# Fused rotation and DiT block on one core: the Exp table load moves by ten slots, V's zeroing moves to GpSimd, the gates' rows are spread by DMA

## The chip, the core and the metric

The kernel runs on one NeuronCore of a Trainium2 chip. The metric is device time in microseconds of one launch, taken several times; the median counts. A profiled execution of the same program is read beside it.

## What is computed

```python
# L0: x (2,1024,288), cond (2,288)
U, _ = qr(P)                                   # (288,64)
R = expm(skew(silu(cond) @ W.T + b))           # (2,64,64)
x = x + (z @ R - z) @ U.T                      # z = x @ U
# L1: a transformer block modulated by the same cond
ada = silu(cond) @ ada_w + ada_b               # (2, 6*288)
shift_msa, scale_msa, gate_msa, shift_mlp, scale_mlp, gate_mlp = split(ada, 6)
x = x + gate_msa * (attention(modulate(layernorm(x), shift_msa, scale_msa)) @ proj_w + proj_b)
x = x + gate_mlp * (gelu(modulate(layernorm(x), shift_mlp, scale_mlp) @ fc1_w + fc1_b) @ fc2_w + fc2_b)
```

In the attention each token is a set of 16 heads of 18 channels, and the softmax runs over the 16 heads of the same token (`nthd,ntkd->nthk`), so attention mixes heads within a token and no tokens with each other.

## The kernel before, in words

All five engines run lists written out by hand, tied by semaphores; each engine works its list strictly in order. The program has these stages.

- **Prologue (0 to about 107 us).** A loop of steps k builds the orthogonal basis pivot by pivot (VectorE's reciprocal, L1271, and two updates, L1273 and L1276; ScalarE's square root, L1037, and the scaled row, L1040), then the matrix exponential. Into the same steps "fillers" are laid: TensorE transposes of X, and the products `ada 0` and `ada 1` that give the modulation and the two gates; `fill_out` (L999) is ScalarE's copy of a filler's result out of PSUM, and counts `fill_done`. `ada 1` leaves the gates in `AD[:, 1, :]`: rows 0 and 1 the attention gate of the two batch rows, rows 32 and 33 the MLP gate. GpSimd splits the weights into f16 pairs meanwhile (L460 to L472) and then waits.
- **Rotation and first norms (107 to 120 us).** `delta` (L714) adds the rotation to X, VectorE takes mean and variance (L1319, L1321).
- **qkv (about 120 to 214 us).** NCH = 4 chunks of 512 tokens, NQ = 12 units each, so 48 units; a loop over slots `gu` runs on TensorE, ScalarE and VectorE, in the same order on each. In slot gu: `turn` pieces of the next chunk where TURN_AT says so (slots 5 to 7 for chunk 1, 14, 16, 18 for chunk 2, 26, 28, 30 for chunk 3): TensorE transposes (L739), ScalarE writes them twice (L1081, f32 and f16), VectorE subtracts (L1373, `split`). Then the unit itself: 7 matmuls (L815), ScalarE's copy `high` (L1098 or, for V, L1093), VectorE's remainder `low` (L1419). TensorE's unit gu waits for `low(gu-2)`. Then the slot's `job`s: 16 small matmuls (L799, L776) that turn the unit's heads, copied out by ScalarE (L1114, L1112); job i waits for the copy of job i-2. From slot 24 on, every third slot has a `maxima` (L763) with VectorE's reduction (L1378). Slots 31 to 34 and 37 to 40 have jobs; 35 has none and 36 has one short one (L769 on TensorE, L1105 on ScalarE). VectorE also makes `norm_var` (L1327), `norm_scales` (L1335 to L1343) and `source` (L1352, L1357: the normalised X) of the coming chunk: for chunk 1 in slots 0 to 3, and `turn(1)` in slot 5 waits for it.
- **The gates, before.** In slots 1 to 4 `gate` (L595) spreads one row of AD over 128 partitions by a matmul with a broadcast column of the identity, and `fill_out` copies and scales it (L1006): GATE0 (attention, two batch rows), then GATE (MLP). As soon as the two GATE0 copies are done, GpSimd folds the gate into proj's weights: WP, seven instructions for each batch row (L501 to L507), then GB2 (L513, L514). The projection (about 284 us) is the first reader of WP; GATE itself is first read by `result` (L1550) in the MLP.
- **The Exp table, before.** At `EXP_TABLE_AT` = 2 * NQ + 1 = 25 ScalarE applies Exp to one column (L1136) so that its table is loaded ahead of the softmax. It comes after the slot's jobs.
- **Attention (214 to 284 us).** Scores (L856), Exp (L1142), values (L893). V's groups lie in VG, the first 2048 columns of `scratch`, where the unused columns are zero and one column of each group is 1. VectorE zeroes it (L1450, L1452) after the last `low`; ScalarE's first copy into it (`v_out(0)`, L1151) waits for that. XN, the normalised X that `turn` reads, lay in the same place.
- **Projection, MLP (284 to 419 us).** L947, then L970 and L986, with TensorE busy nearly throughout.

SyncE issues all DMAs in one list: the loads, the 32 small copies that build the skew matrix, the broadcast of fc2's bias (L389, 144 KB from one DRAM row to 128 partitions, after a wait for `weights` 5), then the attention maxima and the outputs.

Of the kernel before, what the change touches and what calls it, by code (L numbers as in the profile page):

```python
# [6 lines left out]
F32 = mybir.dt.float32  # L7
# [5 lines left out]
B, T, D = 2, 1024, 288  # L13
R = 64
H, DH = 16, 18
MLP = 4 * D
P = 128
# [14 lines left out]
def build(nc, x, c, pmat, wskew, bskew, qkv_w, qkv_b, proj_w, proj_b, fc1_w, fc1_b, fc2_w, fc2_b, ada_w, ada_b, out):  # L32
    with ExitStack() as ctx:
# [131 lines left out]
        YT = big[:, 2 * (NF + 1) * CH:2 * (NF + 1) * CH + 6 * D].rearrange("p (a n) -> p a n", a=6)  # L165
        B2ALL = stage[:, NT * D:NT * D + D]
        GB2 = scratch[:, 8704:8704 + B * D].rearrange("p (b n) -> p b n", b=B)
        vd = nc.dram_tensor("skew_entries", [B, NSKEW], F32, kind="Internal").ap()


        in_p, in_c, in_w, in_br, in_ada, in_adab = (sem(n) for n in ("in_p", "in_c", "in_w", "in_br", "in_ada", "in_adab"))
        in_b2, x_bias = sem("in_b2"), sem("x_bias")
        in_wq, in_wp, in_w1, in_w2 = (sem(n) for n in ("in_wq", "in_wp", "in_w1", "in_w2"))
        in_x = [sem(f"in_x{i}") for i in range(NCH)]
        consts = sem("consts")
# [57 lines left out]
        ZT_AT = 34  # L233
        ADA_ROWS = ((0, 1, 3, 4), (2, 5))
        FG = len(work) - 1
        NFILL = FG + 5
        XDONE = [work.index((i + 2, 2)) + 1 for i in range(2)]
        pieces = []
        for n, w in enumerate(work):
# [72 lines left out]
        ROWS_LATER, ROWS_BANK = {4: 2, 8: 3}, {4: VB[0], 8: MXB[0]}  # L312
        PAIRED = 10
        DVE_AT = 17
        GATE_AT = 1
        EXP_TABLE_AT = 2 * NQ + 1
        NSLOT = 6 * 2 * NCH + 7 + 4
        assert max(slots) < NSLOT

# [27 lines left out]
        def _(sp):  # L347
# [39 lines left out]
            sp.wait_ge(weights, 5)  # L387
            src = bass.AP(tensor=fc2_b.tensor, offset=fc2_b.offset, ap=[[0, P], [1, D]])
            sp.dma_start(B2ALL, src).then_inc(in_b2, 16)  # L389

            def max_row(n):
                if n < 2:
# [18 lines left out]
        def _(pool):  # L411
# [83 lines left out]
                pool.memset(HT[96:P, a_, 4, :], FINE).then_inc(ht_ones, 1)  # L495
                pool.wait_ge(ht_ones, a_ + 1)
            pool.wait_ge(in_wp, 96)
            pool.wait_ge(fill_done, FG + 3)
            for b in range(B):
                r = slice(0, 98)  # L500
                chain(pool.tensor_tensor(WPG[:, 0:2, :], SWP[:, 0:2, :], GATE0[:, b, :].unsqueeze(1).broadcast_to([P, 2, D]), ALU.mult))  # L501
# [6 lines left out]
                pool.wait_ge(folded, 2 * b + 2)  # L508

            pool.wait_ge(in_b2, 16)  # L510
            pool.wait_ge(fill_done, NFILL)
            for b in range(B):
                chain(pool.tensor_scalar(GB2[:, b, :], GATE[:, b, :], FINE * FINE, None, ALU.mult))  # L513
                chain(pool.tensor_tensor(GB2[:, b, :], GB2[:, b, :], B2ALL, ALU.mult))  # L514
            for t in range(NT):
                pool.wait_ge(proj_mul, t + 1)
                pool.tensor_tensor(X[:, t, :], X[:, t, :], YT[:, t % 6, :], ALU.add).then_inc(x_mid, 1)  # L517
# [7 lines left out]
        def _(pe):  # L525
# [16 lines left out]
            def filler(n, p_):  # L542
# [42 lines left out]
                                       XT[0:k, b, c0:c0 + 2 * P], start=(b == 0), stop=(b == 2))  # L585
                if pieces[last_piece[n]] == (n, p_):
                    mm.then_inc(fill_ready, 1)

            def gate(n):

                f = MISC
                pe.wait_ge(fill_done, n)
                g, b = divmod(n - FG - 1, 2)
                row = 32 * g + b
                pe.matmul(f[:, 0:D], ident[0:R, row:row + 1].broadcast_to([R, P]), AD[0:R, 1, :], start=True, stop=True).then_inc(fill_ready, 1)  # L595

            def skew_matrix():

# [182 lines left out]
            def job(i):  # L781

                if i == 0:
                    pe.wait_ge(att_const, 1)
                    pe.wait_ge(fill_done, NFILL)
                if i >= 2:
                    pe.wait_ge(col_done, i - 1)
                out = CB[i % 2]
                if jobs[i][0] == "max":
                    max_turn(out, jobs[i][1]).then_inc(col_ready, 1)  # L790
                    return
                pr, w, q = jobs[i]
                pe.wait_ge(qk_low, 6 * pr + 3 + w + 1)
                if w == 2:
                    mm = v_columns(out, pr, q)
                else:
                    for hh in range(4):
                        for c_ in range(2):
                            mm = pe.matmul(out[R * c_:R * c_ + R, P * hh:P * hh + P], HQ[:, 2 * (pr % 2) + c_, w, 4 * q + hh, :],  # L799
                                           ident16[:, :], start=True, stop=True)  # L800
                mm.then_inc(col_ready, 1)
# [28 lines left out]
            for gu in range(NSLOT):  # L830
                n, m = divmod(gu, NQ)
                if n < NCH:
                    if m in TURN_AT[n]:
                        turn(n + 1, (TURN_AT[n].index(m),))
                    qkv(gu)
                for i in slots.get(gu, ()):
                    job(i)
                if gu in AHEAD:
                    maxima(AHEAD[gu])
                if n + 2 < NCH and m in DELTA_AT[n]:  # L840
                    delta(TPC * (n + 2) + DELTA_AT[n].index(m))
                if GATE_AT <= gu < GATE_AT + 4:
                    gate(FG + 1 + gu - GATE_AT)

            def scores(s_):

# [148 lines left out]
        def _(act):  # L995
# [2 lines left out]

            def fill_out(n):  # L999
                act.wait_ge(fill_ready, n + 1)  # L1000
                f = FILL[n % 2] if n <= FG else MISC
                if n > FG:
                    g, b = divmod(n - FG - 1, 2)
                    if n == FG + 1:
                        act.wait_ge(weights, 4)
                    cp = act.mul(GATE[:, b, :], f[:, 0:D], 1.0 / (FINE * FINE)) if g else act.mul(GATE0[:, b, :], f[:, 0:D], FINE)  # L1006
                elif work[n] == "P'":
                    cp = act.copy(PT2[:, :], f[:, 0:D])
                elif work[n] == "mod":

# [8 lines left out]
                elif work[n][0] == "a":  # L1019
                    g = int(work[n][-1])  # L1020
                    rows = 32 * len(ADA_ROWS[g])
                    cp = act.copy(AD[0:rows, g, :], f[0:rows, 0:D])
                else:
                    i, b = work[n]
                    if b < 3:
                        k = BLK[b][1]
                        cp = act.copy(XT[0:k, b, CH * i:CH * i + CH], f[0:k, :])
                    else:
                        act.wait_ge(v_all, 1)
                        cp = act.mul(ZT[:, CH * i:CH * i + CH], f[:, :], 1.0 / RANGE)  # L1030
# [90 lines left out]
            for gu in range(NSLOT):  # L1121
# [6 lines left out]
                    norm_root(1)  # L1128
                for i in slots.get(gu, ()):
                    job_out(i)  # L1130
                if GATE_AT <= gu < GATE_AT + 4:
                    fill_out(FG + 1 + gu - GATE_AT)
                if m == 2 * TPC and n + 2 < NCH:
                    norm_root(n + 2)
                if gu == EXP_TABLE_AT:
# [74 lines left out]
        def _(dve):  # L1210
# [235 lines left out]
                    if m in (2 * TPC + 2, 2 * TPC + 3):  # L1446
                        source(n + 2, 0, (range(0, 2), range(2, 4))[m % 2])

            dve.wait_ge(split_done, 3 * NCH)
            dve.memset(scratch[:, 0:4 * CH], 0.0).then_inc(vg_clear, 1)  # L1450
            dve.wait_ge(vg_clear, 1)
            dve.memset(VG.rearrange("p a c g d -> p (a c g) d")[:, :, DH:DH + 1], 1.0).then_inc(vg_clear, 1)  # L1452

            def normalise(w):

                n, q = divmod(w, 2)
# [88 lines left out]
            def result(n, j):  # L1545
                t = TPC * (n - 2 * NCH) + j
                dve.wait_ge(fc2_ready, t + 1)
                if t >= 6:
                    dve.wait_ge(y_out[t % 6], 16 * (t // 6))
                dve.tensor_tensor(YT[:, t % 6, :], YB[t % 2][:, 0:D], GATE[:, t // 8, :], ALU.mult).then_inc(y_mul, 1)  # L1550
                dve.wait_ge(y_mul, t + 1)
                dve.wait_ge(x_bias, t + 1)
                dve.tensor_tensor(YT[:, t % 6, :], YT[:, t % 6, :], X[:, t, :], ALU.add).then_inc(y_ready, 1)
# [29 lines left out]
```

## Time and profile before

| | before |
|---|---|
| median of 3 runs | 421.26 us (420.74 to 435.42) |
| profiled execution | 420.82 us, of which span 419.1 us |
| TensorE busy | 395.0 us (94%), mean granted clock 0.986 |
| VectorE busy | 275.3 us (66%) |
| ScalarE busy | 229.5 us (55%) |
| GpSimd busy | 116.2 us (28%) |

The span is the time from the first to the last instruction in the trace. Of the three runs two lie at 420.74 and 421.26, and the profiled execution is at 420.82; the third, 435.42, is far from them. Times in the trace are microseconds from the span's start. Engines are PE (TensorE), PEld (its weight load), ACT (ScalarE), DVE (VectorE), POOL (GpSimd), SP (SyncE).

### The profile page before, as it was taken

Reading aid. Unit: us, or ns where it says so; the run is one execution under the profiler, and the core shown is the slowest. Engines: PE = TensorE matmul, PEld = TensorE weight load, DVE = VectorE, ACT = ScalarE, POOL = GpSimd, SP = SyncE. Lnnn points to the kernel's source line nnn. Section 1 sums busy time; section 2 is a strip of 40 time slices with the busy share of each in tenths; the row PEclk is TensorE's granted clock in tenths of the full one; section 3 lists DMA queues with packets and bytes.
Section 4 is the critical chain, followed back from the end, with each engine's and each line's share of the span. In section 5 each row is a group of like instructions: output and inputs, shape, how many; then the busy total and the mean of one; then the engine's idle time right before and its main releaser. Section 6 shows DMA issues by size and latency. Waiting matters only on the chain.

```text
span 419.1 us, 11790 instructions
## 1 busy us (share of the span) xinstructions
PE 395.0 (94%) x4807; PEld 256.2 (61%) x4807; DVE 275.3 (66%) x781; ACT 229.5 (55%) x481; POOL 116.2 (28%) x139
## 2 busy tenths in 40 slices
PE   8999999999989899899979888889999999999996
PEld 4665555666545566667656556568655575666575
DVE  2688885677689856446557256666899776746452
ACT  3356434532267899898877775666775442322200
POOL 6019999973009700000000000006510010101040
PEclk9999999999999999899989899999999999999999
DMA  5999000000000000000000000000000000000011
GB/s 168 300 312 290 21 4 3 1 16 2 2 0 2 2 2 3 3 2 5 2 5 7 3 3 3 2 3 2 2 0 1 16 30 14 29 14 23 21 45 42
DMA packets 7928, 14.72 MB, mean 35 GB/s; under 512 B 2555, under 2 KB 6239, under 8 KB 7748
## 3 DMA queue, kind: packets, MB, share of 16 engines
q1 hardware_dynamic: 7874, 13.96, 11.0%
q8 instruction: 38, 0.62, 0.6%
q14 instruction: 16, 0.13, 0.1%
HBM read 11.52 MB, written 2.38 MB: 33 GB/s over the span
## 4 chain that ended last, share of the span: by engine, by line
PE 65%; DVE 16%; ACT 11%; issue 7%; ACTq 0%; DVEq 0%
PE psum L986 11%; PE psum L528 8%; PE psum L970 8%; PE psum L815 6%; ACT scratch L1081 3%; PE psum L799 3%; PE psum L893 3%; PE psum L628 2%; DVE BN L1319 2%; ACT big L1114 2%; PE psum L640 2%; PE psum L909 2%; DVE scratch L1352 2%; PE psum L584 2%; PE psum L619 2%
## 5 line engine op out<-in xcount | busy, mean ns | idle before, releaser
L970 PE MATMUL psum<-scratch,W 128*128 128x512 f16 (+1 forms) x252 | 57.9, 379 | 0.0
L986 PE MATMUL psum<-W,big 128*128 128x288 f16 x432 | 55.1, 286 | 0.0
L517 POOL TENSOR_TENSOR X<-X,big 128x288 f32<-128x288 f32 x16 | 13.0, 823 | 148.0 <-ACT big L1179 147.6
L1204 ACT ACTIVATE big<-psum 128x512 f32<-128x512 f32 x36 | 21.3, 597 | 57.0 <-PE psum L970 51.9
L815 PE MATMUL psum<-WQ,scratch 128*128 128x288 f16 (+1 forms) x336 | 49.9, 290 | 1.8 <-DVE scratch L1373 0.9
L986 PEld LDWEIGHTS psum<-W,big 128*128 128x128 f16 x432 | 42.2, 98 | 12.9
L528 PE MATMUL psum<-ident 128*32 128x192 f32 (+3 forms) x146 | 44.1, 386 | 0.0
L1142 ACT ACTIVATE big<-psum 128x1024 f32<-128x1024 f32 x32 | 32.8, 1030 | 17.9 <-PE psum L856 17.7
L970 PEld LDWEIGHTS psum<-scratch,W 128*128 128x128 f16 (+1 forms) x252 | 24.7, 98 | 25.6
L815 PEld LDWEIGHTS psum<-WQ,scratch 128*128 128x128 f16 (+1 forms) x336 | 30.2, 99 | 13.3 <-DVE scratch L1373 1.6
L1081 ACT ACTIVATE scratch<-psum,MOD 128x512 f32<-128x512 f32 (+3 forms) x48 | 34.3, 773 | 6.6 <-PE psum L739 4.0
L522 POOL TENSOR_TENSOR X<-X,scratch 128x288 f32<-128x288 f32 x16 | 13.5, 854 | 84.0 <-DVE big L1534 84.0
L1114 ACT CAST big<-psum 128x512 f16<-128x512 f32 x64 | 34.4, 596 | 0.1
L1040 ACT ACTIVATE scratch<-psum,scratch 64x65 f32<-64x65 f32 x63 | 19.5, 309 | 26.7 <-DVE scratch L1276 26.7
L1532 DVE TENSOR_SCALAR big<-big 128x512 f16<-128x512 f32 x36 | 15.6, 435 | 26.9 <-ACT big L1204 26.8
L1534 DVE SCALAR_TENSOR_TENSOR big<-big 128x512 f16<-128x512 f32 x36 | 26.4, 732 | 1.2
L1037 ACT ACTIVATE scratch<-scratch 64x1 f32<-64x1 f32 x63 | 12.8, 202 | 25.5 <-DVE scratch L1271 24.8
L1373 DVE TENSOR_TENSOR scratch<-scratch 128x512 f16<-128x512 f32 (+1 forms) x24 | 17.6, 731 | 13.1 <-ACT scratch L1081 12.9
L799 PE MATMUL psum<-ident,stage 128*64 128x128 f16 x512 | 22.4, 225 | 3.6 <-ACT big L1114 2.7
L893 PE MATMUL psum<-big,scratch 128*32 128x128 f32 x512 | 23.1, 293 | 2.7 <-ACT scratch L1159 1.4
L1098 ACT ACTIVATE stage<-psum 128x576 f16<-128x576 f32 x32 | 20.9, 654 | 6.4 <-PE psum L815 5.8
L1378 DVE TENSOR_REDUCE MX<-psum 128x16 f32<-128x1024 f32 x16 | 19.5, 1220 | 7.2 <-PE psum L763 7.2
(221 smaller groups left out, 766.0 us busy)
## 6 DMA issues: line engine op xcount, KB each, us to landing
X<-in_x_dram SPq DMA_DIRECT2D x4, 576.0 KB, 17.9
out_dram<-big SPq DMA_DIRECT2D x16, 144.0 KB, 1.7
big<-in_L_cond_W_dram SPq DMA_DIRECT2D x1, 2268.0 KB
big<-in_L_cond_ada_w_dram SPq DMA_DIRECT2D x2, 864.0 KB, 18.4
stage<-in_L_cond_fc_w_dram SPq DMA_DIRECT2D x1, 1296.0 KB, 18.7
big<-in_L_cond_fc_w_dram SPq DMA_DIRECT2D x1, 1152.0 KB
stage<-in_L_cond_qkv_w_dram SPq DMA_DIRECT2D x1, 864.0 KB
big<-in_L_cond_fc_w_dram SPq DMA_DIRECT2D x3, 144.0 KB
```

Source lines behind the costliest of these rows:

```text
L528: pe.matmul(out[:, 0:cols], left, left[:, 0:1].broadcast_to([P, cols]), start=True, stop=True)
L799: mm = pe.matmul(out[R * c_:R * c_ + R, P * hh:P * hh + P], HQ[:, 2 * (pr % 2) + c_, w, 4 * q + hh, :], ident16[:, :], start=True, stop=True)
L815: mm = pe.matmul(UB[gu % 2][:, 0:D], HT[0:r, n % 2, a_, P * a:P * a + P], WQ[0:r, w_, D * w:D * w + D], start=(p_ == 0), stop=(p_ == 6))
L893: mm = pe.matmul(PO[c_][32 * g:32 * g + 32, P * q:P * q + P], VG[:, w % 2, c_, 4 * q + g, :], E[:, s_ % 2, c_, P * g:P * g + P], start=Tru ...
L970: mm = pe.matmul(FB[idx % 3], W1[0:r, w_, P * m:P * m + P], HT[0:r, n % 2, a_, :], start=(p_ == 0), stop=(p_ == 6))
L986: mm = pe.matmul(YB[t % 2][:, 0:D], g[:, a_, f, cols], W2[:, w_, f, :], start=(f == 0 and a_ + w_ == 0), stop=(f == NF - 1 and w_ == 1))
L1081: act.activation(dst, src, ACT.Identity, scale=MOD[0:rows, 2 * l + 1, b, batch:batch + 1], bias=MOD[0:rows, 2 * l, b, batch:batch + 1]).th ...
L1098: act.mul(dst[:, :, 0:2, :] if w else dst[:, :, 0:3:2, :], src.unsqueeze(2).broadcast_to([P, H, 2, DH]), QSCALE / (FINE * FINE)).then_inc( ...
L1114: act.copy(columns(QKT[pr // 4][:, w, :], 16 * (pr % 4), q), src.rearrange("p (h v m) -> p h v m", h=4, v=32)).then_inc(col_done, 1)
L1142: act.activation(E[:, s_ % 2, :, :], psum[:, 3:5, :] if s_ > PAIRED and s_ % 2 else psum[:, 0:2, :], ACT.Exp, scale=DH ** -0.5 / (QSCALE * ...
L1204: act.activation(G32[:, idx % 2, :], FB[idx % 3], ACT.Gelu, scale=1.0 / (FINE * FINE)).then_inc(gelu_sb, 1)
L1534: dve.scalar_tensor_tensor(out=GT[c_ % 2][:, 1, m, :], in0=G32[:, idx % 2, :], scalar=FINE, in1=GT[c_ % 2][:, 0, m, :], op0=ALU.mult, op1= ...
```

## The change

Three things are changed.

1. `EXP_TABLE_AT` becomes 3 * NQ - 1 = 35.
2. VG is zeroed by GpSimd, after GB2, once the transposes of chunk 3 have read XN (`tr_ready` 12), in place of VectorE after its last `split` and `low`.
3. The gates no longer pass through TensorE in slots 1 to 4. ScalarE copies AD's two gates out of PSUM already scaled (two copies in place of one, in the prologue); SyncE writes the two rows of each to DRAM, waits for both, and reads them back spread over 128 partitions. GpSimd's fold waits for these and for the first three units of qkv (`qk_ready` 3).

```diff
+        gd = nc.dram_tensor("gate_rows", [2, B, D], F32, kind="Internal").ap()
+        gate_out, in_gate = sem("gate_out"), sem("in_gate")
-        GATE_AT = 1
-        EXP_TABLE_AT = 2 * NQ + 1
+        EXP_TABLE_AT = 3 * NQ - 1
@@ sync, after the bias broadcast
+            sp.wait_ge(fill_done, ADA1 + 1)
+            for g in range(2):
+                sp.dma_start(gd[g], AD[32 * g:32 * g + B, 1, :]).then_inc(gate_out, 16)
+            sp.wait_ge(gate_out, 32)
+            for g, dst in ((0, GATE0), (1, GATE)):
+                src = bass.AP(tensor=gd.tensor, offset=gd.offset + g * B * D, ap=[[0, P], [1, B * D]])
+                sp.dma_start(dst.rearrange("p b n -> p (b n)"), src).then_inc(in_gate, 16)
@@ gpsimd
-            pool.wait_ge(fill_done, FG + 3)
+            pool.wait_ge(qk_ready, 3)
+            pool.wait_ge(in_gate, 32)
...
-            pool.wait_ge(fill_done, NFILL)
             for b in range(B):
                 chain(pool.tensor_scalar(GB2[:, b, :], GATE[:, b, :], FINE * FINE, None, ALU.mult))
                 chain(pool.tensor_tensor(GB2[:, b, :], GB2[:, b, :], B2ALL, ALU.mult))
+            pool.wait_ge(tr_ready, 3 * NCH)
+            pool.memset(scratch[:, 0:4 * CH], 0.0).then_inc(vg_clear, 1)
+            pool.wait_ge(vg_clear, 1)
+            pool.memset(VG.rearrange("p a c g d -> p (a c g) d")[:, :, DH:DH + 1], 1.0).then_inc(vg_clear, 1)
@@ tensor
-            def gate(n):
-                f = MISC
-                pe.wait_ge(fill_done, n)
-                g, b = divmod(n - FG - 1, 2)
-                row = 32 * g + b
-                pe.matmul(f[:, 0:D], ident[0:R, row:row + 1].broadcast_to([R, P]), AD[0:R, 1, :], start=True, stop=True).then_inc(fill_ready, 1)
...
-                    pe.wait_ge(fill_done, NFILL)
...
-                if GATE_AT <= gu < GATE_AT + 4:
-                    gate(FG + 1 + gu - GATE_AT)
@@ scalar
-                if n > FG:
-                    ...
-                    cp = act.mul(GATE[:, b, :], f[:, 0:D], 1.0 / (FINE * FINE)) if g else act.mul(GATE0[:, b, :], f[:, 0:D], FINE)
...
-                    cp = act.copy(AD[0:rows, g, :], f[0:rows, 0:D])
+                    if g:
+                        act.mul(AD[0:32, 1, :], f[0:32, 0:D], FINE).then_inc(mod_part, 1)
+                        cp = act.mul(AD[32:64, 1, :], f[32:64, 0:D], 1.0 / (FINE * FINE))
+                    else:
+                        cp = act.copy(AD[0:rows, g, :], f[0:rows, 0:D])
...
-                if GATE_AT <= gu < GATE_AT + 4:
-                    fill_out(FG + 1 + gu - GATE_AT)
@@ vector
-            dve.wait_ge(split_done, 3 * NCH)
-            dve.memset(scratch[:, 0:4 * CH], 0.0).then_inc(vg_clear, 1)
-            dve.wait_ge(vg_clear, 1)
-            dve.memset(VG.rearrange("p a c g d -> p (a c g) d")[:, :, DH:DH + 1], 1.0).then_inc(vg_clear, 1)
...
                 dve.wait_ge(fc2_ready, t + 1)
+                if t == 0:
+                    dve.wait_ge(in_gate, 32)
```

## Rows read from the trace of the kernel before

**Rows 1.** The page: busy time by engine, and the chain's shares by engine.

```profile
PE 395.0 (94%) x4807; PEld 256.2 (61%) x4807; DVE 275.3 (66%) x781; ACT 229.5 (55%) x481; POOL 116.2 (28%) x139
...
PE 65%; DVE 16%; ACT 11%; issue 7%; ACTq 0%; DVEq 0%
```

**Rows 2.** Windows of 1 us: busy of each engine, then PEclk, DMA share, GB/s.

```profile
176.00:177.00 1.00, 1.00 (x35) 0.94 (x34) 0.73 (x2) 0.77 (x2) 0.00 (x0) 0.50 0.00 0
...
179.00:180.00 1.00, 1.00 (x21) 0.83 (x21) 0.87 (x2) 0.99 (x3) 0.00 (x0) 1.00 0.00 0
```

**Rows 3.** Timeline of TensorE, slots 27 and 28: start, us, operation, [idle before, releaser].

```profile
172.00 1.03 PE L815 MATMUL psum<-WQ,scratch 128*128 128x288 f16 x7
174.82 1.12 PE L799 MATMUL psum<-ident,stage 128*64 128x128 f16 x16 [1.79 <-ACT big L1114]
...
177.35 1.72 PE L815 MATMUL psum<-WQ,scratch 128*128 128x288 f16 x7
```

**Rows 4.** Timeline of ScalarE, slots 25 to 28.

```profile
171.16 1.28 ACT L1136 ACT_TABLE_LOAD   x1
...
172.56 1.43 ACT L1081 ACTIVATE scratch<-psum,MOD 128x512 f32<-128x512 f32 x2
...
177.65 1.45 ACT L1081 ACTIVATE scratch<-psum,MOD 128x512 f32<-128x512 f32 x2 [0.88 <-issue]
```

**Rows 5.** The chain that ended last, where it leaves ScalarE in slot 30.

```profile
184.94 0.41 PE psum L799 x8
```

**Rows 6.** Timelines of ScalarE, VectorE and TensorE, slots 35 to 38.

```profile
191.33 0.41 ACT L1093 ACTIVATE scratch<-psum 128x288 f16<-128x288 f32 x1
192.19 0.65 ACT L1098 ACTIVATE stage<-psum 128x576 f16<-128x576 f32 x1 [0.45 <-PE psum L815]
...
193.64 0.65 ACT L1098 ACTIVATE stage<-psum 128x576 f16<-128x576 f32 x1 [0.65 <-PE psum L815]
...
192.87 0.46 DVE L1419 SCALAR_TENSOR_TENSOR stage<-psum,stage 128x288 f16<-128x288 f32 x1 [0.64 <-ACT stage L1098]
193.25 1.22 DVE L1378 TENSOR_REDUCE MX<-psum 128x16 f32<-128x1024 f32 x1
...
194.10 1.03 PE L815 MATMUL psum<-WQ,scratch 128*128 128x288 f16 x7
```

**Rows 7.** Timeline of all engines, slots 1 to 4.

```profile
123.00 1.03 PE L815 MATMUL psum<-WQ,scratch 128*128 128x288 f16 x7
...
123.89 0.17 DVE L1327 TENSOR_SCALAR ST<-MV 128x4 f32<-128x4 f32 x1
...
124.20 0.39 ACT L1006 ACTIVATE big<-psum 128x288 f32<-128x288 f32 x1
...
124.65 0.75 PE L595 MATMUL psum<-big,ident 64*128 64x288 f32 x2 [0.61 <-ACT big L1006]
...
125.71 1.87 DVE L1352 TENSOR_SCALAR scratch<-X,MV,ST 128x288 f32<-128x288 f32 x2
126.01 1.40 POOL L501 TENSOR_TENSOR big<-big 128x576 f32<-128x576 f32 x1 [15.58 <-ACT big L1006]
```

**Rows 8.** Timeline of VectorE, slot 22: the same operation with GpSimd at rest.

```profile
165.68 0.76 DVE L1352 TENSOR_SCALAR scratch<-X,MV,ST 128x288 f32<-128x288 f32 x2
```

**Rows 9.** Timeline of VectorE, end of qkv.

```profile
210.18 1.76 DVE L1450 MEMSET scratch<- 128x2048 f32 x1 [0.38 <-issue]
...
214.90 1.23 DVE L1378 TENSOR_REDUCE MX<-psum 128x16 f32<-128x1024 f32 x1 [2.72 <-PE psum L763]
```

**Rows 10.** Timeline of ScalarE, prologue, around the copy of `ada 1`.

```profile
53.81 0.39 ACT L1022 COPY big<-psum 64x288 f32<-64x288 f32 x1
...
54.90 0.31 ACT L1040 ACTIVATE scratch<-psum,scratch 64x65 f32<-64x65 f32 x1 [0.43 <-DVE scratch L1276]
```

**Rows 11.** DMA issues of the page: operands, count, KB each, us to landing.

```profile
stage<-in_L_cond_fc_b_dram SPq DMA_DIRECT2D x1, 144.0 KB, 2.9
```

**Rows 12.** Groups of instructions of GpSimd, shapes kept apart.

```profile
L495 POOL MEMSET scratch<- 32x512 f16 x2 | 1.0, 519 | 10.6 <-PE psum L696 10.5
```

More of the change, by code:

```diff
@@ L235, in build @@
         FG = len(work) - 1
-        NFILL = FG + 5
+        ADA1 = work.index("ada 1")
         XDONE = [work.index((i + 2, 2)) + 1 for i in range(2)]
@@ L1000, in fill_out @@
                 act.wait_ge(fill_ready, n + 1)
-                f = FILL[n % 2] if n <= FG else MISC
-                if n > FG:
-                    g, b = divmod(n - FG - 1, 2)
-                    if n == FG + 1:
-                        act.wait_ge(weights, 4)
-                    cp = act.mul(GATE[:, b, :], f[:, 0:D], 1.0 / (FINE * FINE)) if g else act.mul(GATE0[:, b, :], f[:, 0:D], FINE)
-                elif work[n] == "P'":
+                f = FILL[n % 2]
+                if work[n] == "P'":
                     cp = act.copy(PT2[:, :], f[:, 0:D])
```

## Prediction

> **What bounds the kernel now.** I read the page first: TensorE is busy 94% of the span and is 65% of the chain that ended last, VectorE 16%, ScalarE 11% [rows 1]. So an edit pays only where the chain leaves TensorE. All three parts of the change act in qkv, and there I looked at one-microsecond windows for TensorE's clock, then at each engine's timeline around the lines that the change touches.
>
> Two places matter. In slot 25 ScalarE loads the Exp table at 171.16 and comes to its next list entry at 172.56, 1.40 us later [rows 4]. TensorE runs unit 27 at 172.00 and then sits idle for 1.79 us, until ScalarE's late copies free a PSUM bank [rows 3]. After that its granted clock is at the lower of its two levels (1.2 in place of 2.4 GHz, 0.50 in the window of 176) and is back by 179 [rows 2]; a unit of seven matmuls takes 1.72 us there against 1.03 [rows 3]. ScalarE in turn idles 0.88 us before the next transposes' copy [rows 4]. The chain comes back to TensorE only at 184.94 [rows 5], behind ScalarE's list.
>
> In slots 1 to 4 the four gate matmuls and their copies lie (one pair takes TensorE 0.75 us, one copy ScalarE 0.39 us [rows 7]). There VectorE is the one that is behind: it must finish statistics, `norm_scales` and `source` of chunk 1 before `turn(1)` in slot 5, and its two tiles at 125.71 take 1.87 us while GpSimd folds [rows 7], against 0.76 us with GpSimd at rest [rows 8].
>
> **Part 1, the load leaves slot 25.** ScalarE is spared 1.40 us at 171.16, and if TensorE doesn't idle there, its clock has no reason to fall, unit 28 takes 1.03, and the 0.88 us of ScalarE's idle time goes as well. ScalarE's list is the limit up to 184.94, so the gain is 1.40 + 0.88 = 2.28 us. If only the load went and the later idle time stayed it would be 1.40. More than 2.28 can't come, since ScalarE then has no gap left before 184.94: what is late next is ScalarE's own work. I take 2.3.
>
> **The load arrives in slot 35.** The same 1.40 us starts behind `high(35)`, at 191.33 + 0.41 = 191.74, so `high(36)` starts at 193.14 in place of 192.19. ScalarE had idled 0.45 us before that copy and 0.65 us before the copy of 193.64 [rows 6]; these cover 1.10, and 0.30 is left at `high(37)`. By VectorE: `high(36)` now ends at 193.79, `low(36)` (0.46) at 194.3, and unit 38, which waits for it and started at 194.10, is 0.2 late; the 1.22 us reduction behind it [rows 6] hands about the same on to unit 39. The least is 0.2; the most is the whole delay of `high(36)`, 0.95. I take 0.3, since two ways of counting agree on it and slot 35 has no jobs to wait for. There is no cover beyond those two gaps: put one slot later, behind a job, the load would cost what it does now.
>
> The Trainium skill, "ScalarE: Activation LUTs", section "What ACT_TABLE_LOAD costs", gives 1283 ns for the load and as much again, 1380 ns, for a drain with each switch. The trace has the 1.28 and not the drain: the copy behind the load starts 1.40 after its start. With the page's 2.66 the place in slot 35 would cost some 1.6 and the sum would be a gain of 0.7, by estimate; the trace decides.
>
> **Part 2, V's zeroing.** VectorE's memset of 1.76 us at 210.18 is followed by 2.72 us of idle time until TensorE brings the first maxima at 214.90 [rows 9]. It is covered whole: removing it gives 0. On GpSimd the nearest row is the memset of 512 elements in 0.52 us [rows 12]; four times as many elements are at most 4 x 0.52 = 2.1 us. It starts when the last transposes of chunk 3 are done, some time after 181, and is needed at about 214: 30 us of slack. What is queued behind it on GpSimd is the X update of the projection at 284. It reads nothing, and in its time VectorE has units, reductions and one `split` to do. Between 0 and 0.5 us; I take 0.
>
> **Part 3, the gates' path.** ScalarE, prologue: one more copy of 0.39 us behind 53.81 + 0.39; the square root that follows starts that much later, but the scaled row at 54.90 waits 0.43 us for VectorE in any case [rows 10]. Cover 0.43, cost 0, and at most 0.39.
>
> SyncE: behind the bias broadcast come two small writes, a wait, and two broadcasts of 288 KB, each twice the 144 KB that took 2.9 us [rows 11]. Twice 5.8 for these, and about as much as one 2.9 for the writes and their wait, make 15 us at most from about 85: gates in place by 100, 20 us before slot 0. The next entry of SyncE is the first row of maxima, after slot 36. Cost 0.
>
> TensorE and ScalarE are spared 4 gate products (1.5 us together) and 4 copies (1.6) in slots 1 to 4. As VectorE is behind there, this becomes idle time: 0 gained. If TensorE were the limit it would be 1.5; the wait for VectorE says it is not, so I count this only in the range.
>
> GpSimd is where it can hurt. Now the fold starts at 126.01, after the second gate's copy [rows 7]. After the change it waits for unit 2. That unit ran 123.00 to 124.03; without the gate before it some 0.2 earlier, so the fold starts at about 124.0. It will then be over 2 us sooner too. VectorE's operations from SBUF to SBUF pay for the overlap: 1.87 - 0.76 = 1.1 us for two tiles when GpSimd's 1.40 us product runs beside them [rows 7, 8]. At present only `source(1)` pays. Then the five small operations of `norm_scales` (from 124.3) meet the first product, and `source` meets a later one: up to 1.4 more at the first, and the tail of the fold off VectorE's back later. I take 0.3 lost here, between -0.5 (fewer collisions at the end) and 1.4.
>
> The Trainium skill, "SBUF — State Buffer", section "Who interferes with whom", says that GpSimd holds a port pair in common with VectorE for a whole instruction and the loser blocks, for VectorE's two-port modes and for two SBUF inputs against a GpSimd instruction that reads. The 1.87 against 0.76 agrees. By it the memset of part 2 would block no two-input operation, which speaks for its 0; and each of the small operations in reach of the fold could wait for one whole product.
>
> VectorE's wait in `result` for the gates' DMAs is met 200 us ahead: 0.
>
> **Sum.** Against the profiled execution: 420.8 - 2.3 + 0.3 + 0.3 = 419.1, of which the span is 417.4 as before with 1.7 around it. The median of the runs, 421.26, lies 0.4 above the profile, and its neighbour 420.74 just under; I forecast 419.1 for the new median.
>
> **Rivals.**
> - *The clock falls in slots 2 to 5.* Without the gates TensorE has nothing between unit 2 and unit 3, and between unit 4 and `turn(1)`, but waits for VectorE, each about 1 us. In slot 27 an idle time of 1.79 came ahead of the fall [rows 3]; here there are several shorter ones. For it: the four products were the filling. Against: the trace shows idle times of 0.6 there already at full clock [rows 7]. Price: two units and two sets of transposes at half clock, 2 x 0.69 + about 1 = 2.4, of which some 0.6 hides behind VectorE: 1.8, to 420.9.
> - *Slot 35 costs what slot 25 did.* The load opens a gap on TensorE and the clock falls again: 2.28 back, so 421.1. Against it: 1.10 us of idle time on ScalarE in just those slots [rows 6].
> - *More comes back.* Either the fold's new place misses `source(1)` (1.1 twice is there to be had), or another of TensorE's falls in the attention doesn't recur: 1.5 to 2.5 more, 417.0.
> - *Slower: the fold catches `norm_var`.* At 123.89 VectorE makes the 4-column operation on which the square root and all of `norm_scales` hang [rows 7]. If GpSimd's 1.40 us product starts before it, it waits 1.4; the edge is only 0.1 us wide, since the fold starts at about 124.0. TensorE then idles over 2 us ahead of unit 3, more than the 1.79 of slot 27, and its clock does fall. Price 1.4 + 2.4 in place of the 0.3 in the sum: 422.6. This decides from the point where `qk_ready` 3 comes before 123.9.
> - *No change at all* would be the case if `turn(3)`'s copies in slots 26 to 30 were the limit by themselves; then 420.8. The idle time of 1.79 speaks against it, and I fold it into the second rival.
>
> **How the numbers follow.** Forecast 0.42 (own range 418.2 to 420.0), clock falls 0.25, slot 35 as dear 0.08, more comes back 0.15, slower 0.10. The range takes the forecast, the first two rivals and most of the fourth: 416.8 to 421.8 leaves out the slower case and the ends. A change of 2% is 8.4 us, about what a measurement of this kernel can tell from no change; no case comes near it, so within 2% has 0.97, faster 0.02, slower 0.01.
>
> **What would show it.** Windows at 171 to 180: PEclk 1.00 all through, TensorE without an idle time over 0.5. The load after `high(35)`, with a gap of some 0.3 on TensorE before units 38 or 39. In slots 1 to 5: L501 at about 124.0, a long L1337 or L1341 in VectorE's list, PEclk either 1.00 or 0.50 at about 127. The memset on GpSimd at about 180 and nothing moving at 210. The gates' DMAs landed by 100. The prediction is wrong if the clock falls in slots 2 to 5, or if the gap at slot 35 is over 1 us.

## The result, and the profile after

The changed kernel takes 417.76 us (median of 4 runs, 417.65 to 418.09); the kernel before takes 421.18 on the same chip. The ratio is 0.9927, 95% interval 0.9899 to 0.9955: faster by 1.9 to 4.3 us, and within the 2% of "same". The forecast was 419.1, in a range of 416.8 to 421.8. The profiled execution has a span of 416.4 and 418.1 in all, 2.7 less than the 420.8 of before. Some executions of most kernels here, the one before among them, take 10 us or more longer; in their profiles this lies ahead of the first unit of qkv, so the ratios leave them out, and such a profile is read from that unit on (its start stands in brackets below).

The page of the changed kernel, the same two lines as in [rows 1]:

```profile
PE 391.4 (94%) x4799; PEld 253.8 (61%) x4799; DVE 272.4 (65%) x779; ACT 228.0 (55%) x478; POOL 118.4 (28%) x141
...
PE 72%; DVE 12%; ACT 10%; issue 6%; ACTq 0%; DVEq 0%
```

TensorE now has 72% of the chain in place of 65. To see where the 2.7 us went I took four marks from TensorE's timeline in every profile: the first unit of qkv, the first scores, the first matmul of the projection, the first of fc1. Their differences, in us:

| kernel | start to first unit | first unit to scores | scores to projection | projection to fc1 | fc1 to the end |
|---|---|---|---|---|---|
| before | 119.92 | 93.23 | 69.35 | 20.50 | 116.10 |
| changed | 120.06 | 91.47 | 68.67 | 20.50 | 115.70 |
| e1, load alone | (133.49) | 90.84 | 67.71 | 20.49 | 116.07 |
| e2, gates and zeroing, load in 25 | (143.02) | 94.52 | 68.15 | 20.49 | 115.72 |
| e3, zeroing alone | 120.52 | 93.22 | 69.26 | 20.50 | 115.70 |
| e4, late fold | 121.17 | 87.61 | 67.72 | 20.49 | 115.71 |
| e5, load in slot 37 | 120.25 | 92.44 | 69.83 | 20.50 | 115.68 |
| e6, load in slot 58 | 120.15 | 91.19 | 69.22 | 20.50 | 115.64 |
| e7, fold in the pause | (136.55) | 87.64 | 69.89 | 20.50 | 115.72 |
| e8, late fold, gates by TensorE | (133.37) | 89.21 | 68.81 | 20.49 | 115.72 |
| e9, as e2 | 119.98 | 92.69 | 69.18 | 20.49 | 115.66 |
| e10, slot 27 filled | 120.34 | 92.17 | 68.73 | 20.50 | 116.06 |
| e11, fold in the pause, GB2 late | (133.67) | 87.62 | 67.77 | 20.50 | 115.74 |
| e12, as e4 | 120.47 | 87.62 | 69.22 | 20.49 | 115.70 |

So of the 2.7 the qkv stage gave 1.76, the attention 0.68, the MLP 0.40, and the prologue took 0.14.

**Slots 25 to 30.** TensorE, ScalarE and the windows of the changed kernel, against [rows 2 to 4]:

```profile
172.73 1.03 PE L819 MATMUL psum<-WQ,scratch 128*128 128x288 f16 x7
174.05 0.90 PE L803 MATMUL psum<-ident,stage 128*64 128x128 f16 x16 [0.28 <-ACT big L1115]
...
175.75 1.02 PE L819 MATMUL psum<-WQ,scratch 128*128 128x288 f16 x7
```

```profile
171.74 1.48 ACT L1082 ACTIVATE scratch<-psum,MOD 128x512 f32<-128x512 f32 x2
...
176.00 1.45 ACT L1082 ACTIVATE scratch<-psum,MOD 128x512 f32<-128x512 f32 x2
```

```profile
176.00:177.00 1.00, 1.00 (x17) 0.69 (x16) 0.66 (x1) 1.00 (x2) 0.00 (x0) 1.00 0.00 0
```

TensorE's idle time is 0.28 in place of 1.79, the clock stays at 2.4 GHz, unit 28 takes 1.02 in place of 1.72, and ScalarE comes to its copy of 176.00 without idling. From the slot-26 transposes' copy to the slot-30 one ScalarE's list has become shorter by 2.46 us, counted from where the load began: 181.94 - 171.16 = 10.78 before, 180.06 - 171.74 = 8.32 after.

**Slot 35.** ScalarE, then TensorE, against [rows 6]:

```profile
189.91 1.28 ACT L1135 ACT_TABLE_LOAD   x1
...
191.31 0.63 ACT L1099 ACTIVATE stage<-psum 128x576 f16<-128x576 f32 x1
191.84 0.26 ACT L1106 ACTIVATE MRT<-psum 64x128 f16<-64x128 f32 x1
192.00 0.63 ACT L1099 ACTIVATE stage<-psum 128x576 f16<-128x576 f32 x1
```

```profile
192.50 1.03 PE L819 MATMUL psum<-WQ,scratch 128*128 128x288 f16 x7
```

The copy behind the load starts 1.40 after it. `high(35)` came 1.85 us sooner than before (189.48 against 191.33), unit 38 only 1.60 sooner (192.50 against 194.10): the load costs 0.25 here.

**Slots 0 to 8.** All engines, against [rows 7]:

```profile
124.17 1.40 POOL L511 TENSOR_TENSOR big<-big 128x576 f32<-128x576 f32 x1 [13.59 <-PE psum L819]
...
124.68 0.91 DVE L1336 TENSOR_TENSOR ST<-ST 128x4 f32<-128x4 f32 x1
...
125.82 0.52 DVE L1340 TENSOR_SCALAR ST<-ST 128x4 f32<-128x4 f32 x1
...
126.95 1.72 DVE L1351 TENSOR_SCALAR scratch<-X,MV,ST 128x288 f32<-128x288 f32 x2
...
127.09 1.03 PE L819 MATMUL psum<-WQ,scratch 128*128 128x288 f16 x7 [1.45 <-DVE scratch L1418]
...
128.96 0.94 DVE L1351 TENSOR_SCALAR scratch<-X,MV,ST 128x288 f32<-128x288 f32 x2
```

The fold starts at 124.17 in place of 126.01. A 4-column product of VectorE, 0.16 by itself, now takes 0.91, and `source(1)` takes 1.72 and 0.94 for its two pairs, where before it took 1.87 and 1.79. TensorE waits 1.45 for `low(2)`.

**V's zeroing and the gates' DMAs.** GpSimd, VectorE and the DMA issues of the changed kernel, against [rows 9, 11]:

```profile
180.10 1.81 POOL L525 MEMSET scratch<- 128x2048 f32 x1 [37.70 <-PE psum L744]
```

```profile
213.28 1.23 DVE L1377 TENSOR_REDUCE MX<-psum 128x16 f32<-128x1024 f32 x1 [5.10 <-PE psum L768]
```

```profile
big<-gate_rows SPq DMA_DIRECT2D x1, 288.0 KB, 3.2
GATE<-gate_rows SPq DMA_DIRECT2D x1, 288.0 KB, 3.7
```

The memset takes 1.81 on GpSimd, and VectorE merely idles longer ahead of the first maxima (5.10 in place of 2.72). The broadcasts were issued at 86.1 and 86.5 and landed by 90.3.

### The profile page after: what moved, and what is told of

It reads as the page before. It is cut to its first block, busy times and chain, and to the rows that moved or that the text cites. A ratio compares the mean times of both kernels' runs of the same rounds, so it can differ in the third digit from the quotient of the medians.

```text
span 416.4 us, 11776 instructions
## 1 busy us (share of the span) xinstructions
PE 391.4 (94%) x4799; PEld 253.8 (61%) x4799; DVE 272.4 (65%) x779; ACT 228.0 (55%) x478; POOL 118.4 (28%) x141
## 4 chain that ended last, share of the span: by engine, by line
PE 72%; DVE 12%; ACT 10%; issue 6%; ACTq 0%; DVEq 0%
PE psum L972 13%; PE psum L988 13%; PE psum L541 9%; PE psum L819 5%; ACT scratch L1082 3%; PE psum L803 3%; PE psum L895 3%; ACT big L1115 3%; PE psum L633 2%; PE psum L949 2%; PE psum L645 2%; PE psum L597 2%; PE psum L624 2%; PE psum L911 2%; PE psum L637 1%
```

## The experiments

**e1: the table load alone.** The kernel before with one line changed:

```diff
-        EXP_TABLE_AT = 2 * NQ + 1
+        EXP_TABLE_AT = 3 * NQ - 1
```

> The kernel before with the table load alone moved to slot 35. My theory (the load's move is the whole gain, 2.3 back in slots 25 to 30, 0.3 paid in slot 35): about 2.0 to 2.5 us faster than before, span near 417, the clock at its upper level from 171 to 180. Rival (the gates' way through DMA is what pays): within 0.5 us of before. Second rival (the load alone saves only its own 1.4): 1.1 faster.

Ratio 0.9967 (0.9937 to 0.9997), or 1.4 us with an interval of 0.1 to 2.7. In the profile the qkv stage is 90.84, 2.39 less than before and 0.63 *less* than the changed kernel's. The windows at the place (13 us later here) show the clock up:

```profile
189.00:190.00 1.00, 1.00 (x21) 0.70 (x19) 0.47 (x1) 1.00 (x2) 0.00 (x0) 1.00 0.00 0
```

In the profiles, the load's move is more than the whole gain of the qkv stage, and what was added to it costs 0.63. The times of whole runs don't show e1 ahead: its ratio of 0.9967 lies above the changed kernel's 0.9927, and the intervals overlap a little. The profiles have e1 0.63 shorter in qkv and 0.37 longer in the MLP, so 0.26 is left between the two apart from the attention, where e1's own profile, at 67.71, is among the shortest.

**e2 and e9: gates and zeroing, load back in slot 25.** The changed kernel with that line set back, run twice.

```diff
-        EXP_TABLE_AT = 3 * NQ - 1
+        EXP_TABLE_AT = 2 * NQ + 1
```

> The changed kernel with the table load put back in slot 25: gates by DMA and V's zeroing on GpSimd alone. My theory: these two cost up to 0.7 us by slot 25 (the fold starts 2 us sooner and meets the small operations of norm_scales) and give nothing back, so 0 to 0.7 slower than before. Rival (the eight operations taken from TensorE and ScalarE pay): 1 to 1.5 faster than before.

> The same kernel as in the second run (gates by DMA, V's zeroing on GpSimd, load in slot 25), for a profile in which nothing else disturbs the qkv stage. From the first unit to the first scores the kernel before took 93.2 us, the load moved alone 90.8 and the changed kernel 91.5; so my theory is 93.2 + 0.6 = 93.9. Rival (the second run's 94.5 is the true price, and the parts don't add): 94.5.

e2's ratio is 1.0002 (0.9975 to 1.0028): no change, as my theory had it, and not the 1 to 1.5 faster of the rival. In its profile qkv takes 94.52, and the clock falls in two places of it: once behind the load, as before, and once in slots 5 to 7, behind the wait of 1.45. TensorE, then windows, in e2 (23 us later here):

```profile
150.05 1.03 PE L819 MATMUL psum<-WQ,scratch 128*128 128x288 f16 x7 [1.45 <-DVE scratch L1418]
```

```profile
151.00:152.00 1.00, 1.00 (x6) 0.52 (x5) 1.00 (x3) 0.65 (x1) 0.88 (x2) 0.85 0.00 0
152.00:153.00 1.00, 0.72 (x3) 0.27 (x3) 0.97 (x3) 0.00 (x0) 0.95 (x1) 0.50 0.00 0
```

Up to slot 24 e2's lists are those of the changed kernel, and it has the same waits of TensorE, 0.7 and 1.45, ahead of units 3 and 4. So this is the prediction's first rival, come true in another execution: five profiles have these slots (changed, e2, e5, e6, e9), each with the wait of 1.45, and the clock fell in one. Against e9, the same kernel, e2's matmuls run 23.04 us later up to unit 4, 23.98 later in the slots ahead of the load's gap and 24.87 later at the first scores: the first fall cost 0.94, the second 0.89. e9 gave 92.69, where I had expected 93.9: a miss that tells something. TensorE, then windows, in e9:

```profile
172.60 1.03 PE L819 MATMUL psum<-WQ,scratch 128*128 128x288 f16 x7
175.42 0.90 PE L803 MATMUL psum<-ident,stage 128*64 128x128 f16 x16 [1.79 <-ACT big L1115]
...
177.12 1.02 PE L819 MATMUL psum<-WQ,scratch 128*128 128x288 f16 x7
```

```profile
176.00:177.00 1.00, 1.00 (x43) 0.87 (x44) 0.56 (x2) 1.00 (x3) 0.00 (x0) 1.00 0.00 0
177.00:178.00 1.00, 1.00 (x10) 0.70 (x8) 1.00 (x1) 1.00 (x2) 0.00 (x0) 1.00 0.00 0
```

The idle time behind the load is the same 1.79 us as before [rows 3], with the same work around it, and the clock did *not* fall. So that gap puts the clock at risk; it doesn't bring it down each time. Of the four profiles with it (before, e2, e3, e9) three show the fall, and of the ten without it none shows one in slots 25 to 30. Without the fall, e9 and the changed kernel differ by the load's place alone: 92.69 - 91.47 = 1.22.

**e3: the zeroing alone.** The kernel before with VectorE's four lines moved into GpSimd's list, behind GB2.

```diff
@@ gpsimd
+            pool.wait_ge(tr_ready, 3 * NCH)
+            pool.memset(scratch[:, 0:4 * CH], 0.0).then_inc(vg_clear, 1)
...
@@ vector
-            dve.wait_ge(split_done, 3 * NCH)
-            dve.memset(scratch[:, 0:4 * CH], 0.0).then_inc(vg_clear, 1)
...
```

> The kernel before with V's zeroing alone moved to GpSimd. My theory: VectorE's memset was covered by idle time, so no change, within 0.3 us, with VectorE idle for 1.8 us more ahead of the first maxima of the attention. Rival (GpSimd's memset holds up VectorE near slot 30, or VectorE was late at the end of qkv): 0.5 or more either way.

Ratio 0.9995 (0.9975 to 1.0016), and qkv 93.22 against 93.23: nothing there, as predicted. The MLP is 0.40 shorter in the profile (115.70 against 116.10); the account of the prediction comes back to it.

**e10: TensorE kept busy in slot 27.** The kernel before, with spare matmuls into a free bank:

```diff
@@ tensor, behind qkv(gu)
+                if gu == 27:
+                    pe.wait_ge(cast_done, 9)
+                    for _ in range(5):
+                        clock(bank[0], ident[:, :], 2 * P)
```

> The kernel before, with five spare matmuls of 256 columns in slot 27 on TensorE, where it idled 1.79 us behind the load; the load stays in slot 25. They write a free bank and nothing is computed with them. If the clock falls because of the idle time, it stays at its upper level from 171 to 180, ScalarE's 0.88 us of idle time goes, and qkv takes about 92.3 us against 93.2; the rest of the 2.4, some 1.4, is the load's own. Rival (the clock falls for another reason, or its fall costs nothing): 93.2 or more.

```profile
173.26 2.34 PE L528 MATMUL psum<-ident 128*128 128x256 f32 x10
175.53 0.64 PE L799 MATMUL psum<-ident,stage 128*64 128x128 f16 x16
...
176.96 1.02 PE L815 MATMUL psum<-WQ,scratch 128*128 128x288 f16 x7
```

```profile
176.00:177.00 1.00, 1.00 (x43) 0.86 (x39) 0.78 (x2) 1.00 (x3) 0.00 (x0) 1.00 0.00 0
```

The load is where it was, the gap is filled, the clock stays up, and qkv takes 92.17: 1.06 of e1's 2.39 were the clock's fall, and the other 1.33 is the load's own time in slot 25 less what it costs in slot 35. As e9 shows, one such profile by itself wouldn't prove that the filling kept the clock up. The price of the fall, about 1.1 (0.89 in e2), comes out twice more, from e9: 93.23 + 0.63 - 92.69 = 1.17 in qkv, and on ScalarE's list, from the load's start to the slot-30 copy, 10.78 before against 9.68 (171.76 to 181.44) in e9, so 1.10.

**e5 and e6: other places for the load.** The changed kernel with the load in slot 37, and in the last slot.

```diff
-        EXP_TABLE_AT = 3 * NQ - 1
+        EXP_TABLE_AT = 3 * NQ + 1        # e5
+        EXP_TABLE_AT = NSLOT - 1         # e6, = 58
```

> The changed kernel with the table load two slots later, in slot 37, behind that slot's unit and two jobs. My prediction said that behind a job the load would cost what it did in slot 25: about 2 us slower than the changed kernel, a gap of over 1 us on TensorE and its clock lower after it. Rival (from slot 31 on ScalarE has idle time in every third slot, so any slot there is cheap): within 0.5 us of the changed kernel, without a fall of the clock.

> The changed kernel with the load in the last slot, 58, behind ScalarE's last eight copies of qkv. TensorE waits for just those copies there, so nothing covers it: my theory is a cost of 1.0 to 1.4 us against the changed kernel at the start of the attention. Rival (the first scores are enough to cover it): no change.

e5: ratio to before 0.9935 (0.9859 to 1.0010), qkv 92.44, so 0.97 slower than in slot 35 and not the 2 that I had said. ScalarE, then TensorE, in e5:

```profile
193.57 1.28 ACT L1135 ACT_TABLE_LOAD   x1
```

```profile
195.90 0.90 PE L803 MATMUL psum<-ident,stage 128*64 128x128 f16 x16 [0.91 <-ACT big L1115]
```

Behind the jobs the load opens a gap of 0.91 us on TensorE: with the 0.25 of slot 35 the direct cost is 0.97 + 0.25 = 1.22, where slot 25 has 1.22 + 0.25 = 1.47 without the clock (e9). The clock stayed up in this profile.

e6: ratio 0.9929 (0.9837 to 1.0020). TensorE in e6, at the start of the attention:

```profile
214.52 0.61 PE L858 MATMUL psum<-big 63*128 63x128 f16 x8 [1.49 <-ACT big L1141]
...
215.63 1.08 PE L895 MATMUL psum<-big,scratch 128*32 128x128 f32 x16
```

TensorE waits 1.49 there, but in the changed kernel it waits 0.77 for VectorE's reduction at the same place, so part of the load is covered. From the first unit to the first values product e6 takes 215.63 - 120.15 = 95.48, the changed kernel 215.12 - 120.06 = 95.06: slot 58 is 0.4 dearer than slot 35, where I had expected 1.0 to 1.4, and not free as the rival had it.

**e4, e12: the fold later.** The changed kernel with one number changed:

```diff
-            pool.wait_ge(qk_ready, 3)
+            pool.wait_ge(qk_ready, 15)
```

> The changed kernel with the fold started after unit 14 (qk_ready 15) in place of unit 2, when VectorE is no longer the engine that is behind. My theory (GpSimd's products stretch VectorE's operations in slots 0 to 8 and those are on the chain): the tiles of source(1) go back to 0.76 us a pair, norm_scales to 0.2 each, and the kernel is 2 to 3 us faster than the changed one. Rival (TensorE's and ScalarE's own order limits these slots): less than 0.7 faster. Second rival: the fold now collides with source(3) and the gain is given back.

> The late fold again, as the version that may beat both, for a firmer ratio: 5 to 6 us faster than before (ratio about 0.987), qkv 87.6 from first unit to first scores. A rival would be that its one series had luck with the clock in the attention: ratio 0.99 or more.

e4: ratio to before 0.9863 (0.9831 to 0.9895); e12: 0.9836 (0.9800 to 0.9872), median 415.56. VectorE and GpSimd in e12:

```profile
125.08 0.16 DVE L1336 TENSOR_TENSOR ST<-ST 128x4 f32<-128x4 f32 x1
...
126.25 0.76 DVE L1351 TENSOR_SCALAR scratch<-X,MV,ST 128x288 f32<-128x288 f32 x2
...
127.29 0.76 DVE L1351 TENSOR_SCALAR scratch<-X,MV,ST 128x288 f32<-128x288 f32 x2
```

```profile
146.07 1.40 POOL L511 TENSOR_TENSOR big<-big 128x576 f32<-128x576 f32 x1 [35.09 <-PE psum L819]
```

With GpSimd at rest the product takes 0.16 and the pairs 0.76 each. qkv takes 87.62: 3.85 less than the changed kernel, more than the 2 to 3 I had expected. This beats both kernels: the intervals of its two ratios lie below the changed kernel's. The fold now collides with the three `split`s of chunk 2 (1.43, 0.83 and 0.74 in place of 0.69), with `norm_scales` and the first pair of `source(3)`; VectorE has idle time of about 1 us or more ahead of each `split`, and the second rival's price didn't come.

**e8: the late fold with the gates left on TensorE.** The kernel before plus the load in slot 35, the zeroing on GpSimd, and the fold's start:

```diff
             pool.wait_ge(fill_done, FG + 3)
+            pool.wait_ge(qk_ready, 15)
```

> No DMA for the gates: the kernel before (gates by TensorE and ScalarE in slots 1 to 4), with the load in slot 35, V's zeroing on GpSimd and the fold after unit 14. My theory for the changed kernel was that taking the eight operations away gives nothing because VectorE is late there; with the fold gone from these slots VectorE is no longer late, so the four products and copies now count: 0.5 to 1.5 slower than the late fold with the gates by DMA (415.5). Rival (the gates' DMA path gives nothing even then): the same as that, within 0.3.

Ratio 0.9904 (0.9790 to 1.0017), qkv 89.21: 1.59 more than e12, at the upper end of what I expected. TensorE in e8:

```profile
138.10 0.75 PE L600 MATMUL psum<-big,ident 64*128 64x288 f32 x2 [0.61 <-ACT big L1011]
```

Once the fold is out of the way, the gates' products and their waits for ScalarE's copies are what slots 1 to 4 wait for. The DMA path is worth 1.6 us then. The four kernels with the load in slot 35 make a square, by their time in qkv:

| | early fold | fold after unit 14 |
|---|---|---|
| gates by TensorE | 90.84 (e1) | 89.21 (e8) |
| gates by DMA | 91.47 (changed) | 87.62 (e12) |

So moving the fold away gives 1.63 with the gates on TensorE and 3.85 with the gates by DMA, where it also starts about 2 us sooner (124.17 against 126.01). With the early fold the gates' way and the sooner start together cost 0.63; no run has the gates by DMA and the fold still at 126, so how much of it is the one and how much the other isn't shown.

**e7 and e11: the fold in GpSimd's pause.** The seven instructions per batch row moved ahead of `pool.wait_ge(rot_psum, 3)`, and the wait for `qk_ready` taken out; in e11 it stands ahead of GB2:

```diff
@@ gpsimd, e11
-            pool.wait_ge(rot_psum, 3)
...
-            pool.wait_ge(qk_ready, 3)
             pool.wait_ge(in_gate, 32)
...
+            pool.wait_ge(rot_psum, 3)
...
+            pool.wait_ge(qk_ready, 15)
             pool.wait_ge(in_b2, 16)
```

> The changed kernel with the fold ahead of the wait for the rotation, so that it fills GpSimd's pause from about 98 to 113 us; the two memsets of HT come after it, GB2 after them. My theory (collisions with VectorE in slots 0 to 8 are what the fold costs, 2.3 us): nearly all of the 2.3 of the late fold, less what it loses where the rotation's and chunk 0's small SBUF operations stand (105 to 116 us), so 1.5 to 2.3 faster than the changed kernel. Rival (the memsets of HT come too late for unit 0, or norm_scales(0) and source(0) are now the ones held up): 0 to 1 faster.

> The changed kernel with the fold in GpSimd's pause from 98 us on, and GB2 alone after unit 14. With GB2 directly behind the memsets, norm_var and norm_scales of chunk 0 took 0.4 us longer; the theory is that this 0.4 comes back and nothing else moves: qkv 87.6, 10.15 us from the first rotation matmul to the first unit, as fast as the late fold or 0.1 to 0.3 faster. Rival (the pause isn't free: GpSimd's f32 products hold up VectorE in the exponential's and the basis's last steps): slower than the late fold.

e7: ratio 0.9862 (0.9785 to 0.9940), qkv 87.64. From the first rotation matmul to the first unit it took 136.55 - 126.00 = 10.55 us, against 10.15 (119.92 - 109.77) before: GB2 beside chunk 0's `norm_var` and `norm_scales`. So by these two stages it is 3.83 - 0.41 = 3.4 faster than the changed kernel, more than the 1.5 to 2.3 I had expected. e11, with GB2 late, took 133.67 - 123.52 = 10.15 and 87.62: the 0.4 came back. Its four runs lie between 416.36 and 428.51 and give no ratio; I can't say that it beats the late fold.

## Why the prediction was right, point by point

- **The load leaves slot 25: predicted 2.3 (1.40 to 2.28), measured 2.46 on ScalarE's list; with slot 35's price taken off, predicted 2.0, measured 2.39 (e1).** The mechanism held in both parts: the load's own time, and the idle time that the low clock had made. On ScalarE's list they are 9.68 - 8.32 = 1.36 (e9 against the changed kernel) and 1.10 (before against e9). "More than 2.28 can't come" was 0.2 too tight: the fall cost ScalarE 1.10, of which its idle time of 0.88 was only a part.
- **The load in slot 35: predicted 0.3, measured 0.25**, by the two idle times of [rows 6]. That behind a job it would cost what it does now was half wrong: in slot 37 it costs 0.97 more, the direct part, without the clock.
- **The table load's drain.** The Trainium skill ("ScalarE: Activation LUTs", "What ACT_TABLE_LOAD costs") adds 1380 ns of drain to each switch of tables; the trace after has the next operation 1.40 behind the load's start, as before. The trace decides. The estimate by that page, a gain of 0.7, was also added up wrongly: with the 0.3 of part 3 it is 0.4, and it charged the drain to slot 35 without taking it off slot 25.
- **V's zeroing: predicted 0, measured 0 in qkv** (e3), and the memset 1.81 where I had at most 2.1. For the whole kernel the 0 isn't shown: the 0.40 of the MLP, below, goes with it.
- **The prologue's extra copy: predicted 0, at most 0.39.** ScalarE in the changed kernel, against [rows 10]:

```profile
54.38 0.40 ACT L1021 ACTIVATE big<-psum 32x288 f32<-32x288 f32 x1
54.81 0.20 ACT L1038 ACTIVATE scratch<-scratch 64x1 f32<-64x1 f32 x1
55.05 0.31 ACT L1041 ACTIVATE scratch<-psum,scratch 64x65 f32<-64x65 f32 x1
```

  The cover of 0.43 is used up to the last: the scaled row starts 1.43 after the one before it (53.62 to 55.05), as against 1.42 (53.48 to 54.90); its idle time ahead is gone.
- **Gates by DMA: predicted in place by 100, measured by 90.3.** The 5.8 for each broadcast was a bound; they took 3.2 and 3.7.
- **Taking the eight operations out gives 0, the sooner fold costs 0.3 (-0.5 to 1.4): measured 0.63 together** (changed kernel against e1). The fold started at 124.17, as forecast, `norm_var` at 124.03 got away by 0.14 us, and `norm_scales` was caught: 0.91 where 0.16 is enough. The 0.63 is inside the range, but its two terms aren't shown apart, and the 0 for the eight operations holds at most beside the fold: with the fold late they are worth 1.59 (e8 against e12). What I under-sized is the fold: moving it away gives 1.63 with the gates on TensorE (e1 to e8) and 3.85 without them (changed to e12). "At present only `source(1)` pays" was wrong: before, the second and third `split` of slots 5 to 8 took 1.39 and 1.08, in the changed kernel the three take 1.24, 1.19 and 0.95, and in e12 0.69, 0.67 and 0.68. The Trainium skill's rule in "SBUF — State Buffer", "Who interferes with whom" (two SBUF inputs wait for a GpSimd instruction that reads, one-input operations outside the two-port modes don't) agrees with the 0.91 for the product and with the 0.17 of the reciprocal ahead of it, which ran while the same GpSimd product did.
- **No fall of the clock in slots 2 to 5 in the changed kernel's profile**, though TensorE waited 1.45 us there. That is luck in part: e2, with the same lists up to slot 24, shows the fall. The rival had 0.25, and one profile in five has it. Its price of 1.8 was too high: the fall cost 0.94 there.
- **What the sum left out: 0.68 in the attention and 0.40 in the MLP.** The first is in the rival "more comes back". The clock was low in the attention twice before (by the windows, some 216.3 to 219.7 and 233.4 to 236.8) and once, twice as long, after (213.3 to 220.1). Where it never was, the attention took 67.7 to 67.8 us (e1, e4, e11), with one fall 68.2 to 69.3, with two 69.4 to 69.9. It varies between profiles of one kernel: e4 has none and 67.72, e12 one and 69.22. So I count the 0.68 as luck of a profile, not as the change's doing.
- The 0.40: TensorE waits 0.31 for `source` ahead of a transpose in the MLP in each of the three kernels profiled with VectorE's zeroing (before, e1, e10: 116.06 to 116.10), and doesn't in the eleven with GpSimd's (115.64 to 115.74). The delay starts nine microseconds sooner, in VectorE's list. VectorE before, then the same entries in e3 (0.50 later there):

```profile
322.97 0.18 DVE L1321 BATCH_NORM_AGGREGATE MV<-BN 128x2 f32<-128x6 f32 x1
323.40 0.46 DVE L1319 BATCH_NORM_STATS2 BN<-X 128x6 f32<-128x288 f32 x1 [0.25 <-DVE MV L1321]
```

```profile
323.46 0.18 DVE L1325 BATCH_NORM_AGGREGATE MV<-BN 128x2 f32<-128x6 f32 x1
323.56 0.44 DVE L1323 BATCH_NORM_STATS2 BN<-X 128x6 f32<-128x288 f32 x1
```

  Before, e1 and e10 have this pause of 0.25 between two entries of VectorE, with no other engine to wait for in the profile, and none of the eleven others has it. What the zeroing changes for VectorE here is only that its list is shorter by the two memsets and their waits; why the pause goes with it stays open.

With the attention and the MLP left out the sum stands at 1.62 (1.76 - 0.14) against a forecast of 1.7, which leans on two misses that cancel: 0.4 more from the load than forecast, 0.3 more lost in slots 0 to 8. The median moved by 3.4, to 417.76: that is outside my own range for the forecast (418.2 to 420.0) and nearest to the rival "more comes back", so the mechanism of qkv was right and the rest of the gain isn't its doing. The 2.7 of the profiles lies below the 3.4, within the ratio's interval; no run says where the difference comes from.

## What to carry to other kernels

Ask of an engine's idle time who it is waiting for, then look at what a *third* engine does to that one: here two engines' work was cut by 3 us in slots where VectorE was late, and together with a fold that started sooner this lost 0.63; moving GpSimd's work out of VectorE's way then gave 3.85, and with it away the same cut was worth 1.6. A fixed cost such as a table load goes where its engine has idle time on either side of the next item, ahead of the jobs that others wait for; the same 1.4 us cost 0.25 in slot 35, 1.2 in slot 37 and, in slot 25, 1.5 without and about 2.5 with the clock's fall. And price a gap on TensorE twice, for itself and for the clock, the second only with a chance.

## What was not expected of the hardware

- The same idle time of 1.79 us on TensorE, with the same matmuls before and after, was followed by 1.2 GHz in the kernel before, in e2 and in e3, and by 2.4 GHz throughout in e9. A wait of 1.45 us was followed by 1.2 GHz in e2 and left the clock up in the changed kernel, e5, e6 and e9, with the same lists around it. One of 0.91 (e5) left it up.
- A fall costs 0.9 to 1.2 us in qkv (e2, e9, e10). In the attention profiles with one fall are 0.4 to 1.6 us longer than those without, and with two 1.6 to 2.2.
- GpSimd's products stretch even VectorE's smallest operations: 4 columns, 0.16 us alone, 0.91 beside a product of 1.40.
- VectorE pauses 0.25 us between two of its own entries at one place of the MLP in all three kernels with two more memsets in its list, and in none of the eleven without.
